# One-layer macaron block with 16-head attention on one core: two heads per TensorE tile, two-bank units, eight heads per accumulator

## The reference

```python
x = x + 0.5 * ffn(layernorm(x), W1, b1, W2, b2)      # relu(x @ Wq1.T + b1) @ Wq2.T + b2
q = rope(h @ Wq.T + bq); k = rope(h @ Wk.T + bk)     # h = layernorm(x), 16 heads of 8
v = h @ Wv.T + bv
attn = softmax(q @ k.T / sqrt(8))                    # per head 512 x 512
x = x + (attn @ v) @ Wo.T + bo
x = x + 0.5 * ffn(layernorm(x), W1, b1, W2, b2)      # the same weights again
```

## Time and profile before

| | us |
|---|---|
| runs of the kernel before | 629.36, 630.07, 634.07 (median 630.07) |
| profiled execution, first to last instruction | 629.4 |
| its PE busy | 577.3 |
| its DVE busy | 488.3 |
| its ACT busy | 365.1 |
| its POOL busy | 180.8 |

### The profile page before, as it was taken

How to read it: one execution, slowest core, us unless ns; L and a number is a source line. 1 busy time by engine, 2 the same in 40 slices (tenths; PEclk the granted TensorE clock), 3 DMA queues, 4 the chain that set the end, 5 groups by cost and what they waited for, 6 DMA issues and landing times. The chain is left out here.

```text
span 629.4 us, 11175 instructions
## 1 busy us (share of the span) xinstructions
PE 577.3 (92%) x3412; PEld 263.1 (42%) x3412; DVE 488.3 (78%) x1098; ACT 365.1 (58%) x693; POOL 180.8 (29%) x209
## 2 busy tenths in 40 slices
PE   3867979999999999999999999999999899998985
PEld 2545443423444434443535344444444234423444
DVE  6463959899888988889798979898888787887022
ACT  1211028666767675767676766667676657676822
POOL 6120008102910273006510661038102810102000
PEclk9988889999999999999999999999999989999999
DMA  7012211221121122112211212121211121100000
GB/s 232 3 38 84 74 41 59 65 76 57 43 81 54 56 67 64 41 56 71 68 59 50 76 51 76 38 72 45 85 51 67 49 72 65 56 7 1 2 18 17
DMA packets 20946, 35.96 MB, mean 57 GB/s; under 512 B 4144, under 2 KB 11824, under 8 KB 20912
## 3 DMA queue, kind: packets, MB, share of 16 engines
q1 hardware_dynamic: 20240, 35.01, 17.9%
q10 hardware_dynamic: 672, 0.52, 0.3%
HBM read 22.55 MB, written 8.39 MB: 49 GB/s over the span
## 5 line engine op out<-in xcount | busy, mean ns | idle before, releaser
L666 ACT ACTIVATE probs<-scores_T 128x512 f32<-128x512 f32 x512 | 290.8, 598 | 160.8 <-PE scores_T L492 159.8
L763 DVE TENSOR_REDUCE maxima<-scores 128x1 f32<-128x512 f32 x512 | 326.8, 681 | 58.9 <-PE scores L483 57.3
L483 PE MATMUL scores<-k_stack,q_stack 72*128 72x512 bf16 x512 | 194.6, 389 | 8.5 <-DMA k_stack<-k_scratch 4.3
L492 PE MATMUL scores_T<-q_stack,k_stack 75*128 75x512 bf16 x512 | 187.5, 384 | 8.5 <-ACT probs L666 3.8
L502 PE MATMUL heads_acc<-probs,v_heads 128*32 128x512 f32 x1024 | 136.9, 608 | 2.0 <-ACT heads L673 1.5
L483 PEld LDWEIGHTS scores<-k_stack,q_stack 72*128 72x128 bf16 x512 | 50.4, 98 | 123.0 <-DVE maxima L763 60.7
L492 PEld LDWEIGHTS scores_T<-q_stack,k_stack 75*128 75x128 bf16 x512 | 48.4, 98 | 86.5 <-ACT probs L666 57.5
L557 PEld LDWEIGHTS side<-w_q,hidden 128*128 128x128 f32 x512 | 65.7, 192 | 9.5 <-ACT hidden L656 1.4
L557 PE MATMUL side<-w_q,hidden 128*128 128x128 f32 x512 | 66.5, 275 | 1.2 <-ACT hidden L656 1.1
L566 PE MATMUL heads_acc<-ones_f 128*128 128x256 bf16 x274 | 44.9, 308 | 11.9 <-DVE thr L811 10.9
L656 ACT ACTIVATE hidden<-side,b_col 128x512 f32<-128x512 f32 x64 | 43.9, 690 | 12.0 <-PE side L551 11.7
(11 more groups left out here) (94 smaller groups left out, 494.7 us busy)
## 6 DMA issues: line engine op xcount, KB each, us to landing
q_stack<-q_scratch SPq DMA_DIRECT2D x32, 288.0 KB
k_stack<-k_scratch SPq DMA_DIRECT2D x96, 96.0 KB
k_scratch<-k_parts SPq DMA_DIRECT2D x8, 384.0 KB, 3.4
q_scratch<-q_parts SPq DMA_DIRECT2D x8, 384.0 KB, 3.4
resid<-in_x SPq DMA_DIRECT2D x8, 256.0 KB, 5.3
k_swap<-k SPq DMA_DIRECT2D x16, 128.0 KB, 2.7
q_swap<-q SPq DMA_DIRECT2D x16, 128.0 KB, 2.0
out_y<-resid SPq DMA_DIRECT2D x8, 256.0 KB, 2.0
```

The lines of the kernel that those rows point to most:

```text
L483: pe.matmul(scores[:, bank_of(n, NSC), :], q_stack[0:ROWS, s, t * P:(t + 1) * P], k_stack[0:ROWS, s, :], start=True, stop=True).then_inc(s ...
L492: pe.matmul(scores_T[:, bank_of(n, NST), :], k_stack[0:ROWS + PARTS, s, t * P:(t + 1) * P], q_stack[0:ROWS + PARTS, s, :], start=True, sto ...
L666: act.activation(probs[:, s % (2 * QUAD), t, :], scores_T[:, bank_of(n, NST), :], ACT.Exp, scale=SCALE).then_inc(s_exp, 1)
L763: dve.tensor_reduce(maxima[:, c:c + 1], scores[:, bank_of(s * T + t, NSC), :], AX_X, ALU.max)\
```

## The change

The hardware loop and its tables go; all steps are written out. The new names:

- q and k are split into two float32r parts instead of three bf16 parts. Four products of 8 rows make 32 rows, one or three more subtract the maximum. One head's rows start at partition 0, a second head's at partition 64 (`e` = 0, 1). Each matmul uses half of TensorE's rows; two heads' matmuls stand one behind the other and write two banks of one `unit`.
- Three units of two banks take the place of the five banks of scores. Maxima and exponentials use them in turn, and each DVE or ACT instruction handles two banks (128 x 1024). A batch has 32 steps of such a pair (`STEPS`); the maxima run `LEAD = 12` steps ahead. One side bank is left.
- `values` accumulates eight heads in one accumulator, in 16 partitions of results each, one burst of four heads after every second step. POOL's spreading of v goes: DVE writes the biased v directly.
- POOL takes `split_max` (2 operations instead of DVE's 5) and the layer norm's application (L726 before) from DVE, and in the prologue q's rotation.
- The stacks are double buffered by batch. Their DMAs are issued for a whole batch at once (in the prologue: the first four heads, then the rest). The fills of constant rows become DMAs from ACT's queue.

```diff
-NST = 2
-NSC = 3
-LEAD = 7
-PARTS = 3
-ROWS = PARTS * PARTS * DH
+PARTS = 2
+PROD = PARTS * PARTS * DH
+ROWS_MAX = PROD + 1
+ROWS_EXP = ROWS_MAX + PARTS
+STEPS = NPAIR * T
+LEAD = 12
+RING = 4
+UNITS = 3
...
+SIDE = {
+    0: ("attn_T", 0, "proj"), 1: ("k", 0, "proj"), 2: ("q", 0, "proj"),
+    3: ("heads_T", 1, "post"), 4: ("v", 0, "proj"), 5: ("max_T", 1, "core"),
...
+    13: ("max_T", 2, "core"),
...
+    20: ("ffn2_up", 0, "post"), 21: ("max_T", 3, "core"),
...
-        q_stack = sb("q_stack", [P, H, S], BF16)
+        q_stack = sb("q_stack", [P, 2, NPAIR, S], F32R)
...
-        scores_T = psum("scores_T", [P, NST, S])
-        scores = psum("scores", [P, NSC, S])
+        unit = psum("unit", [P, UNITS, 2, S])
...
+            def stack(j, hs, landed):
+                for n in "qk":
+                    sp.wait_ge(s_scratch[n], (j + 1) * 16 * PARTS)
+                wait(sp, s_scoresT, (j - 1) * STEPS)
+                for e in range(2):
+                    for c in range(PARTS):
+                        rows_c = slice(64 * e + PARTS * DH * c, 64 * e + PARTS * DH * (c + 1))
+                        part = scratch["q"][j % 2, c, e, :, hs, :].rearrange("d h t -> d (h t)")
+                        part = bass.AP(part.tensor, part.offset, [[0, PARTS]] + [list(y) for y in part.ap])
+                        sp.dma_start(q_stack[rows_c, j % 2, hs, :].bitcast(F32).rearrange("p h t -> p (h t)"),
+                                     part).then_inc(landed, 16)
+                        parts = scratch["k"][j % 2, :, e, :, hs, :].rearrange("c d h t -> c d (h t)")
+                        sp.dma_start(k_stack[rows_c, j % 2, hs, :].bitcast(F32).rearrange("p h t -> p (h t)"),
+                                     parts).then_inc(landed, 16)
...
+            stack(0, slice(0, 2), s_stack_first)
+            stack(0, slice(2, NPAIR), s_stack[0])
+            max_row(0)
+            for b in range(B + 1):
+                if on("proj", b):
+                    swap("k", b + 1)
+                    swap("q", b + 1)
+                if b < B:
+                    max_row(b * NQ + 1)
+                if on("proj", b):
+                    to_scratch("k", b + 1)
+                    to_scratch("q", b + 1)
+                if b < B:
+                    max_row(b * NQ + 2)
+                if on("proj", b):
+                    stack(b + 1, slice(0, NPAIR), s_stack[(b + 1) % 2])
...
+            def scores_of(k):
...
+                if r == 0:
+                    pe.wait_ge(*stacked(*divmod(quad, NQ)))
+                if (free := unit_free(max_use(k))) is not None:
+                    pe.wait_ge(*free)
+                to = unit_of(max_use(k))
+                for e in range(2):
+                    part = slice(64 * e, 64 * e + ROWS_MAX)
+                    mm = pe.matmul(to[:, e, :], q_stack[part, quad // NQ % 2, pair, t * P:(t + 1) * P],
+                                   k_stack[part, quad // NQ % 2, pair, :],
+                                   start=True, stop=True)
+                mm.then_inc(s_scores, 1)
...
+            for n in range(ALL_STEPS + 2):
+                if n < ALL_STEPS:
+                    scores_T_of(n)
+                scores_of(n + LEAD)
+                if n < ALL_STEPS:
+                    side_work(side_of(*divmod(n, STEPS)))
+                if n >= PV_LAG and (n - PV_LAG) % 2 == 0:
+                    values((n - PV_LAG) // 2)
...
-                dve.tensor_reduce(maxima[:, c:c + 1], scores[:, bank_of(s * T + t, NSC), :], AX_X, ALU.max)\
+                dve.tensor_reduce(maxima[:, quad % 2, :, r], unit_of(max_use(k)), AX_X, ALU.max).then_inc(s_max, 1)
...
-                act.activation(probs[:, s % (2 * QUAD), t, :], scores_T[:, bank_of(n, NST), :], ACT.Exp,
+                act.activation(probs[:, burst % RING, 2 * pp:2 * pp + 2, :], unit_of(exp_use(n)), ACT.Exp,
```

More of the change, by code:

```diff
@@ L79 @@
[L79 to L127, removed]
@@ new lines, with on, side_of, heads_copied_at @@
+STATS = {0: ("ffn1", "ffn1"), 9: ("ffn2", "post"), 18: ("attn", "ffn1")}
+def on(kind, b):
+    return {"ffn1": b + 2 < B, "proj": b + 1 < B, "post": b > 0, "core": b < B}[kind]
+def side_of(b, n):
+    name, arg, kind = SIDE.get(n, (None, None, None))
+    if name is None or not on(kind, b):
+        return None
+    if name == "max_T":
+        quad = b * NQ + arg
+        return (name, 0, quad, 0) if quad < ALL_QUADS else None
+    return (name, arg, b + AHEAD[kind], 0)
+def heads_copied_at(b, n):
+    if n == 2 and b > 0:
+        return b * 2 - 1
+    if n == 18 and b < B:
+        return b * 2
+    return None
@@ L156, in wait, with user_of @@
+def user_of(use):
+    if use < LEAD:
+        return "max", use
+    n, half = divmod(use - LEAD, 2)
+    if n < ALL_STEPS - LEAD:
+        return ("max", n + LEAD) if half else ("exp", n)
+    return "exp", use - LEAD - (ALL_STEPS - LEAD)
 def wait(engine, semaphore, value):
-    if not isinstance(value, int) or value > 0:
+    if value > 0:
         engine.wait_ge(semaphore, value)
[L162 to L170, removed]
@@ L304, in macaron_layer, with bank_of, tokens_of, unit_of @@
         s_stored = sem("y_stored")
[L307 to L320, removed]
+        def bank_of(b):
+            return side[:] if b == 0 else unit[:, UNITS - 1, b - 1, :]
+        def tokens_of(b):
+            return bank_of(b).rearrange("p (t d) -> p t d", t=T)
+        def unit_of(use):
+            return unit[:, use % UNITS, :, :]
+        def unit_free(use):
+            if use < UNITS:
+                return None
+            what, n = user_of(use - UNITS)
+            return (s_max if what == "max" else s_exp), n + 1
+        def bank_taken(name, arg, index, _):
             if name == "max_T":
@@ new lines, in values @@
+            def values(burst):
+                quad, kt = divmod(burst, T)
+                b, g = divmod(quad, NQ)
+                half, odd = divmod(g, 2)
+                pe.wait_ge(s_exp, 2 * (burst + 1))
+                if kt == 0 and not odd:
+                    pe.wait_ge(s_v, b + 1)
+                    wait(pe, s_heads, quad // 2)
+                for j in range(QUAD):
+                    at = (kt * 2 + half) * QUAD + j
+                    mm = pe.matmul(heads_acc[32 * j:32 * j + 32, :], v_heads[:, b % 2, at, ODD * odd:ODD * odd + 32],
+                                   probs[:, burst % RING, j, :], start=(kt == 0 and not odd), stop=(kt == T - 1 and odd == 1))
+                mm.then_inc(s_pv, 1)
@@ new lines, in _ @@
+            for k in range(LEAD):
+                max_of(k)
+            for n in range(ALL_STEPS):
+                b, step = divmod(n, STEPS)
+                max_of(n + LEAD)
+                side_part(side_of(b, step))
+                which, kind = STATS.get(step, (None, None))
+                if which is not None and on(kind, b):
+                    ln_stats(which, b + AHEAD[kind])
+            for use in EPILOGUE:
+                side_part(use)
+                if use[0] == "out":
+                    ln_stats("ffn2", B - 1)
```

677 lines of the change are left out of this document (284 added, 393 removed), and 14 rows, old and new, of the table SIDE.

## The result

The changed kernel takes 889.38 us (median of four runs, 886.00 to 893.48) where the kernel before takes 629.73 (629.36 to 634.07): 1.41 times as long, with a 95% interval of 1.4009 to 1.4168. The forecast was 865, in a range of 790 to 955. The profiled execution took 886.0, its span is 884.2. The runs of e4, e5, e8, e9 and e10 spread by 2 to 7% with their mean granted clock (e5: 0.903 to 0.928, the kernel before: 0.96 to 0.98), so e5 and the runs built on it are compared by batches of their traces that stayed at full clock.

A forecast was written before the change was run, and what follows sets the result against it. PE sets the pace, but waits for stack DMAs on two engines: 97 us to the first exponentials + 7 batches x 98 + 56 for the last batch + 26 at the end = 865 us, range 790 to 955.

The forecast's parts named there:

- The mechanism: Stack DMAs run on two engines, so PE, in order, waits at step 20 of seven batches, some 36 us each.
- Transfer 47.4: A batch's stack: 1.05 MB on each of two DMA engines at 23.3 GB/s plus 2.4 fixed, 47.4 us.
- Stall 36.4: PE's wait for the next stack at step 20: issue at 26 plus transfer 47.4 minus 37.0, 36.4 us per batch.
- Period 98: Batches 0 to 6: 26 + 47.4 + 12 steps x 1.85 + 2 for the clock, 98 us each.
- The pair, 0.22 predicted: Two heads' score matmuls on PE run side by side in 0.22 us, a gain of 14.1 us per batch.
- The first rival: A pair's two heads run one after the other on PE: 83 us more, 948 us; chance 0.23.
- Mode changes, 0.24 per round trip: Switching PE's tile shape between scores and side work costs 30 x 0.24 = 7.2 us per batch.
- Units, DVE and ACT: DVE under 52.8 us per batch, ACT at most 45, both under PE; three units alone do not bind.
- POOL, 12 applications x 0.297: Layer norm applications moved to POOL add 3.6 us per batch; POOL stays near 23.
- The prologue, -9.3 and -3: Normalisations moved to POOL save 9.3 us, q's rotation there about 3; first stack issued at 42.6 us.
- The turning point: The change becomes faster with a stall under about 12 us per batch: transfer under 23 us, five engines or more.
- the second rival: Stack DMAs spread over 8 engines or more, stall under 3 us or none: 575 us; chance 0.12.

The follow-up runs named there:

- e4: The changed kernel with 230 filler matmuls on PE ahead of each batch's wait for the stack; 872.56 us.
- e5: e1 with each stack DMA writing every second of 32 partitions instead of 16 neighbours; 637.48 us beside 630.44 for the kernel before.
- e8: e5 with the DMAs that fill the constant rows issued by SP after its loads instead of by ACT; 632.39 us.
- e9: e5 with each maximum taken over half of its columns and the exponent's scale at a tenth; 629.93 us.
- e10: e7 with each maximum taken over half of its columns and the exponent's scale at a tenth; 613.22 us.
- e1: The changed kernel with stack rows reordered so that all stack DMAs' source patterns begin with 8 instead of 2; 722.16 us, 1.143 times the kernel before.
- e6: The changed kernel with 280 filler matmuls on PE ahead of each batch's wait for the stack; 868.39 us, 1.375 times the kernel before.
- e7: e5 with score matmuls reading only the upper 16 bits of each float32r part, as bf16; 617.19 us, 0.9755 times the kernel before.
- e11: e7 with the DMAs that fill the constant rows issued by SP instead of ACT; 617.43 us, 0.977 times the kernel before.
- e2: The changed kernel with sixteen stack DMAs of 8 rows per batch, source beginning with 4; 860.04 us, 1.359 times the kernel before.

## Why the prediction was right, and where it was not

**The mechanism holds.** PE waits at step 20 of batches 0 to 6 for the stack, on two engines, with all queued behind it. e1 and e5 show it by taking the wait away in two parts: 889 to 722 to 637 us.

**Its terms, each within a few us.** Issue of the stack, predicted 26 us after the batch's first step: 29.0 (431.73 against 402.75), since a step takes 2.08 us and not 1.85. Transfer 47.4: 41.8 in the first batch, since an engine moves 26 GB/s and not 23.3. Stall 36.4: 28.6 in the mean (26.1 to 29.9). Longer steps gave cover, the faster transfer shortened it. From the stack's landing to the next batch, with the clock's loss, 24.2: 26.9 at least (1.7 and the 25.2 of e6's comparison), 28.5 in the mean. Period 98: 99.1, which is (797.02 - 103.06) / 7. So that the period came out within 1 us was luck: its errors cancelled, the issue 3 us late, the transfer 5.6 short, the rest 4.3 long, most of it the clock's (5.2 where 2 was priced).

**The sum.** 6 us are missing in the prologue (103.06 against 97), 8 in seven periods, 5 from the last batch's start to the end (87.2 against 82), and 1.8 lie outside the span: 865 + 21 = 886.

**The pair, 0.22 predicted.** It was mis-sized: 0.33, 7 us per batch. The first rival (0.44) falls as a mechanism, since e7's pair of bf16 takes 0.24. The step that failed is "I take 0.22, since both parts are rounded to a short form first". The rounding doesn't make the instruction cheap; its operand type does. A weight load of the scores has a median of 98 ns before, 183 to 187 in the changed kernel and 93 in e7. e7 changes the loaded and the streamed operand together, so which of the two costs the 0.09 is not shown.

**Mode changes, 0.24 per round trip.** Nearly: 0.19 around eight `side` entries and 0.13 around four transposes. In e7 entering costs 0.08 more (0.32 against 0.24), 0.27 in all around the eight; with float32r that part is hidden in the 0.33 of the pair.

The Trainium skill, TensorEngine Tiling (Array Packing), Key Properties, says that a change of tiling mode drains the engine. The rows are in line with it, and its price here is 0.1 to 0.3 us.

**Units, DVE and ACT.** Right: DVE 47.3 per batch (under 52.8), ACT 41.5 (at most 45), and both stay under PE. That DVE doesn't bind is shown (e9, e10); ACT's load was not varied.

**POOL, 12 applications x 0.297.** Wrong by 2.7 times: 795 ns each, POOL at 29.9 per batch. Beside work all the same, but not in the prologue.

**The prologue, -9.3 and -3.** This step failed: the issue was forecast at 42.6 and came at 53.17. The prediction took away DVE's 10.46 us beside the memset, and put 1.2 on POOL where it takes 3.13. Above all it didn't count what moved with it: ACT issues the fills, is held for 9.4 us by four issues, and reads its weights only at 12.82 (4.43 before). e8 shows 3.6 us of that; the rest was not taken apart.

**The turning point, "five engines or more", was wrong twice.** e1 has eight engines and a transfer of 21.6 us, under the 23 given, and is still 14% slower. First, the rate per engine falls to 14 to 15 GB/s if the 16 rows are neighbours. Second, an unstalled batch is 65.3 and not 59, so no stall at all can be afforded. For the same reason the second rival's 575 was 62 too low against e5: 9 in the prologue (77.98 against 69), the rest in batches, whose mean is 66.9 ((546.06 - 77.98) / 7), with the falls of the clock in them.

The Trainium skill, DMA: Bandwidth & Descriptors, section "Why a DMA increments its semaphore by 16 and not by 1", gives the engines' number as the prediction used it. The shares of 0.12, 0.25 and 0.50 to 0.58 for leading sizes of 2, 4 and 8 agree.

**Where the intended gain went.** Side by side, the pairs save 64 x 0.11 = 7 us per batch against 128 x 0.22. Dearer `side` work after each change of mode takes 30 x 0.15 = 4.5 of it back. PE is busy 3.9 us less (61.35 against 65.25), and 3.4 of those become waits in PE's own order: 65.3 against 65.8. The fastest versions that take all maxima are e7 and e11, at 0.976 of the kernel before, with half of each part's bits unused; with all bits e5 and e8 are the best, and neither can be told from it.

## What to carry to other kernels

A DMA from DRAM to SBUF is priced by two counts: the engines that its source's leading dimension allows, and the groups of neighbouring partitions that its destination reaches; before a layout is widened, work out both and set the transfer against the steps that cover it. A wait at the head of an in-order engine costs its length and then its clock: here 5 us on top of 29. When a sum comes out right, check its terms; here two of them were off by 6 and 4 us per batch, in opposite directions.

## What the runs showed of the hardware

**The destination's spread limits a stack.** 66 GB/s into 8 neighbouring partitions on four engines (e2), 115 to 131 into 16 on eight (e1), 221 into every second of 32 on the same eight (e5). Per group of four neighbouring partitions that is 33, 29 to 33, and 28 GB/s. In e5 each engine moves 25 GB/s, as the two of the changed kernel do (26), so there the number of engines may be the limit again.

The Trainium skill, SBUF — State Buffer, section "Door 1: The DMA port swizzle (why `[64,N]` ≈ `[32,N]`)", has bandwidth go by how many of 16 ports the partitions reach, four neighbours to one, 435 GB/s in all. An estimate from it is 54, 109 and 218 for the three. e5 agrees, though its eight engines at 26 GB/s would give 208 by themselves; e1 and e2 lie somewhat above, for a reason that no run here shows.

**The clock.** After 26 to 30 us without work PE ran at 1.2 GHz (granted clock 0.50) for another 11 to 33 us with hardly a gap in its work, not for the 5.5 that the earlier trace rows suggested. A short wait can be followed by as much: in e5 and in each of e7 to e11, 1.9 to 3.7 us without work at step 20 of the first batch and then 20 to 34 us at 1.2 GHz; in e5 PE was busy for 29.4 of 31 us there. It falls inside batches as well, with no long wait near: in e5's fourth batch five steps in a row take 16.5 us that take 11.9 in the batches around it. What sets that off stays open, and so does how much of the 2.8 us wait's cost is the clock's.

**Issues can be dear.** Two DMAs that fill one row each from a repeated source hold their engine for 7.16 us on ACT and 6.55 on SP. The two that fill three rows each, from a repeated source too, take 2.21 and 1.70, and a stack DMA 0.6 to 0.7. Why one row costs more than three was not tried.
